# Row maxima of a local attention taken from fp32 scores in 64x96 tiles, in place of bf16 scores in 128x160 tiles

## The reference

```
WINDOW, HEADS, DIM_HEAD, QK_SCALE = 32, 16, 64, 8.0
...
mask = (it < jb) | (it > jb + w) | (jb == -1)
sim = einsum('bhwie,bhwje->bhwij', bq, bk2) * QK_SCALE
sim = where(mask, -finfo.max, sim)
attn = softmax(sim, -1)
out = einsum('bhwij,bhwje->bhwie', attn, bv2)
```

## Time and profile before

| what | value |
|---|---|
| median of 3 runs | 3442.39 us (3433.99 to 3449.18) |
| profiled execution, its own time | 3430.56 us |
| its span | 3428.4 us |
| mean granted TensorE clock | 0.939 |
| PE busy | 3294.6 us, 96% |
| DVE busy | 2253.3 us, 66% |
| ACT busy | 2308.7 us, 67% |
| POOL busy | 1170.0 us, 34% |

### The profile page before, as it was taken

How to read it: one execution, slowest core, us unless ns; L and a number is a source line. 1 busy time by engine, 2 the same in 40 slices (tenths; PEclk the granted TensorE clock), 3 DMA queues, 4 the chain that set the end, 5 groups by cost and what they waited for, 6 DMA issues and landing times.

```text
span 3428.4 us, 55664 instructions
## 1 busy us (share of the span) xinstructions
PE 3294.6 (96%) x17648; PEld 2094.4 (61%) x17648; DVE 2253.3 (66%) x3692; ACT 2308.7 (67%) x3969; POOL 1170.0 (34%) x1073
## 2 busy tenths in 40 slices
PE   5999899999999999999999999999999999999997
PEld 2444466666666666666666666666666666666664
DVE  5654476676666667667667667666766766766763
ACT  2543487777767767767767767777766777766773
POOL 2000143335433336333336333245332344333330
PEclk9965799999999999999999999999999999999997
DMA  2000010011100001100011100011100011100010
GB/s 74 1 1 1 13 44 35 34 41 42 46 36 33 34 35 50 47 30 37 34 37 51 44 33 37 31 43 47 43 33 31 37 47 43 45 31 31 37 36 20
DMA packets 101641, 121.85 MB, mean 36 GB/s; under 512 B 21972, under 2 KB 50770, under 8 KB 101458
## 3 DMA queue, kind: packets, MB, share of 16 engines
q1 hardware_dynamic: 101586, 121.15, 10.1%
HBM read 19.38 MB, written 1.05 MB: 6 GB/s over the span
## 4 chain that ended last, share of the span: by engine, by line
PE 86%; ACT 6%; DVE 5%; issue 3%; DMA 0%; SPq 0%; POOL 0%; DVEq 0%; ACTq 0%; POOLq 0%
PE ring L790 14%; PE ring L812 12%; PE ring L768 5%; PE bank L829 5%; PE ring L788 5%; PE ring L766 4%; PE ring L798 4%; PE ring L778 3%; PE bank L565 3%; PE ring L565 3%; PE bank L736 2%; PE ring L736 2%; PE ring L566 2%; PE ring L567 2%; PE bank L567 2%
## 5 line engine op out<-in xcount | busy, mean ns | idle before, releaser
L506 POOL TENSOR_TENSOR sq_lo<-sq_q,sq_hi 128x512 fp32r<-128x512 f32 x192 | 244.5, 1273 | 1500.0 <-ACT sq_hi L1009 1500.0
L790 PE MATMUL ring<-fin 64*128 64x160 f32 (+1 forms) x3072 | 608.0, 318 | 0.0
L1318 DVE TENSOR_REDUCE neg_max<-ring 128x2 bf16<-128x320 f32 x768 | 357.4, 489 | 265.7 <-PE ring L768 261.7
L812 PEld LDWEIGHTS ring<-probs_t,v_sb 128*128 128x128 f32 x3072 | 468.9, 199 | 72.9 <-issue 33.1
L790 PEld LDWEIGHTS ring<-fin 64*128 64x128 f32 x3072 | 440.5, 188 | 109.6 <-issue 4.8
L812 PE MATMUL ring<-probs_t,v_sb 128*128 128x160 f32 (+1 forms) x3072 | 506.1, 310 | 0.7 <-ACT probs_t L1033 0.7
L1024 ACT ACTIVATE neg_row<-ring 1x512 bf16<-1x512 f32 x384 | 225.1, 586 | 276.5 <-PE ring L778 271.8
L1033 ACT ACTIVATE probs_t<-ring 128x320 f32<-128x320 f32 (+1 forms) x768 | 284.1, 422 | 184.3 <-PE ring L798 184.3
L515 POOL TENSOR_TENSOR rot_k<-tc_k,ts_k 128x512 f32<-128x512 f32 x192 | 259.1, 1350 | 374.4 <-issue 374.4
L1328 DVE TENSOR_TENSOR o_feat<-ring,inv_sums 64x512 f32<-64x512 f32 x384 | 263.7, 687 | 168.4 <-ACT inv_sums L1045 165.5
L515 POOL TENSOR_TENSOR rot_q<-tc_q,ts_q 128x512 f32<-128x512 f32 x192 | 245.2, 1277 | 279.6 <-DMA ts_q<-sr_q 257.6
(11 more groups left out here) (185 smaller groups left out, 6050.3 us busy)
## 6 DMA issues: line engine op xcount, KB each, us to landing
ts_q<-sr_q SPq DMA_DIRECT2D x384, 128.0 KB, 2.0
ts_k<-sr_k SPq DMA_DIRECT2D x384, 128.0 KB, 2.0
w_raw<-in_L_ffn_Wqkv SPq DMA_DIRECT2D x48, 192.0 KB, 2.7
wo_sb<-in_L_ffn_Wo SPq DMA_DIRECT2D x6, 512.0 KB, 3.8
w_raw<-in_L_ffn_W SPq DMA_DIRECT2D x6, 341.0 KB, 3.0
rot_sb<-in_rotary SPq DMA_DIRECT2D x1, 1024.0 KB
out<-x_tok SPq DMA_DIRECT2D x16, 64.0 KB, 1.6
w_sb<-in_L_ffn_W SPq DMA_DIRECT2D x6, 128.0 KB
```

Of the source, the lines that this page charges most:

```text
L506: pool.tensor_tensor(sq_lo[:, i, :], sq[i][:], sq_hi[:, i, :].bitcast(F32), ALU.subtract).then_inc(s_sql[i], 1)
L790: pe.matmul(dst[:, at:at + q], k_fin[rows, p % 2, c * P:(c + 1) * P], q_fin[rows, p % 2, c * P:c * P + q], start=False, stop=False)
L812: mm = pe.matmul(dst[:, c * P:c * P + q], v_sb[:, c, p, h * DIM_HEAD:h * DIM_HEAD + P], probs_t[:, h, c * KEYS:c * KEYS + q], start=(c == ...
L1318: dve.tensor_reduce(neg_max[:, h, 2 * b:2 * b + 2], bank[2 + 2 * h + b][:, 0:2 * KEYS].rearrange("p (c k) -> p c k", c=2), AX_X, ALU.max, ...
```

## The change

The scores for the maxima are made from the fp32 q and k. The two casts and the bf16 copies go, with the semaphore pair `s_16`; `max_scores` waits for `s_fin`. The scores of a head lie in one bank of 384 columns in place of two of 320: each chunk of 128 queries is split into two blocks of 64, the first to output rows 0 to 63, the second to rows 64 to 127, and each block meets only the 96 keys it can see. The mask tensor is rebuilt for that shape, VectorE reduces once per head in place of twice, and `fin` gets 32 zero columns ahead of each k (a memset ahead of the layers).

```diff
@@ shape_constants
-    local = np.stack([np.where(seen & (j >= 0), 0.0, MASKED), np.where(seen, 0.0, MASKED),
-                      np.where(seen, 0.0, MASKED)], 1)
+    local = np.concatenate([np.where(seen & (j >= WINDOW - HALF_P * (i // HALF_P + 2 * c)), 0.0, MASKED)
+                            for c in range(CHUNKS)], 1)
...
@@ buffers (HALF_P = 64, REACH = 96, NEAR = 4 * REACH)
-        fin = sb("fin", [P, 4, TOK])
-        q_fin, k_fin = fin[:, 0:2, :], fin[:, 2:4, :]
-        q16 = sb("q16", [P, 2, TOK], BF16)
-        k16 = sb("k16", [P, 2, WINDOW + TOK], BF16)
+        fin = sb("fin", [P, 4 * TOK + 2 * WINDOW])
+        q_fin = fin[:, 0:2 * TOK].rearrange("p (i t) -> p i t", i=2)
+        k_fin = fin[:, 2 * TOK:].rearrange("p (i t) -> p i t", i=2)
...
@@ max_scores
-                    pe.wait_ge(s_16[0], n + 1)
-                    pe.wait_ge(s_16[1], n + 1)
+                    pe.wait_ge(s_fin[0], n + 1)
+                    pe.wait_ge(s_fin[1], n + 1)
...
-                for b in range(2):
-                    dst = bank[2 + 2 * h + b]
-                    pe.matmul(dst[:, 0:2 * KEYS], eye16, local_mask[:, b * KEYS:(b + 2) * KEYS], start=True, stop=False)
-                    for c in range(2 * b, 2 * b + 2):
-                        mm = pe.matmul(dst[:, (c % 2) * KEYS:(c % 2 + 1) * KEYS], q16[rows, p % 2, c * P:(c + 1) * P],
-                                       k16[rows, p % 2, c * P:c * P + KEYS], start=False, stop=(c % 2 == 1))
-                    mm.then_inc(s_s, 1)
+                pe.matmul(bank[2 + 2 * h][:, 0:NEAR], eye16, local_mask, start=True, stop=False)
+                for c in range(CHUNKS):
+                    for e in range(2):
+                        at = HALF_P * (2 * c + e)
+                        mm = pe.matmul(bank[2 + 2 * h][HALF_P * e:HALF_P * (e + 1), c * REACH:(c + 1) * REACH],
+                                       q_fin[rows, p % 2, at:at + HALF_P], k_fin[rows, p % 2, at:at + REACH],
+                                       start=False, stop=(c == CHUNKS - 1))
+                mm.then_inc(s_s, 1)
@@ turn_max
-                pe.wait_ge(s_mx, 4 * n + 2 * h + 2)
+                pe.wait_ge(s_mx, 2 * n + h + 1)
@@ turned_scores
-                        pe.matmul(dst[:, at:at + q], k_fin[rows, p % 2, c * P:(c + 1) * P],
+                        pe.matmul(dst[:, at:at + q], k_fin[rows, p % 2, WINDOW + c * P:WINDOW + (c + 1) * P],
...
@@ vector engine, ahead of the layers
-            dve.memset(k16[:, :, 0:WINDOW], 0.0).then_inc(v0, 1)
...
+            dve.memset(k_fin[:, :, 0:WINDOW], 0.0).then_inc(v0, 1)
@@ final
-                dst = (q_fin, k_fin)[i][:, p % 2, :]
+                dst = (q_fin[:, p % 2, :], k_fin[:, p % 2, WINDOW:])[i]
...
-                dve.wait_ge(s_fin[i], n + 1)
-                dve.tensor_copy(q16[:, p % 2, :] if i == 0 else k16[:, p % 2, WINDOW:], dst).then_inc(s_16[i], 1)
@@ maxima
-                for b in range(2):
-                    dve.wait_ge(s_s, 4 * n + 2 * h + b + 1)
-                    if b == 0 and not (isinstance(n, int) and n == 0):
-
-                        dve.wait_ge(s_tm, 2 * n - 1 + h)
-                    dve.tensor_reduce(neg_max[:, h, 2 * b:2 * b + 2],
-                                      bank[2 + 2 * h + b][:, 0:2 * KEYS].rearrange("p (c k) -> p c k", c=2),
-                                      AX_X, ALU.max, negate=True).then_inc(s_mx, 1)
+                dve.wait_ge(s_s, 2 * n + h + 1)
+                if not (isinstance(n, int) and n == 0):
+                    dve.wait_ge(s_tm, 2 * n - 1 + h)
+                dve.tensor_reduce(neg_max[:, h, :],
+                                  bank[2 + 2 * h][:, 0:NEAR].rearrange("p (c k) -> p c k", c=CHUNKS),
+                                  AX_X, ALU.max, negate=True).then_inc(s_mx, 1)
```

More of the change, by code:

```diff
@@ L34 @@
 KEYS = WINDOW + P
+HALF_P = P // 2
+REACH = HALF_P + WINDOW
+NEAR = CHUNKS * REACH
 FFN = int(D * 4 * 2 / 3)
@@ L72, in shape_constants @@
     i = np.arange(P)[:, None]
-    j = np.arange(KEYS)[None, :] - WINDOW
-    seen = (j <= i) & (j >= i - WINDOW)
-    local = np.stack([np.where(seen & (j >= 0), 0.0, MASKED), np.where(seen, 0.0, MASKED),
-                      np.where(seen, 0.0, MASKED)], 1)
+    near = (np.arange(P) % HALF_P)[:, None]
+    j = np.arange(REACH)[None, :]
+    seen = (j >= near) & (j <= near + WINDOW)
+    local = np.concatenate([np.where(seen & (j >= WINDOW - HALF_P * (i // HALF_P + 2 * c)), 0.0, MASKED)
+                            for c in range(CHUNKS)], 1)
     key, query = np.arange(P)[:, None], np.arange(KEYS)[None, :]
@@ L79, in shape_constants @@
     causal = np.where(np.arange(P)[None, :] <= i, 0.0, MASKED)
-    masks = np.concatenate([local.reshape(P, -1), turned, turned, causal, np.eye(P), causal.T], 1).astype(np.float32)
+    masks = np.concatenate([local, turned, turned, causal, np.eye(P), causal.T], 1).astype(np.float32)
     eye = np.eye(P, dtype=np.float32)
@@ L118, in build_program @@
         bank += [ctx.enter_context(nc.psum_tensor(f"bank{i}", [P, 512], F32))[:, :] for i in (6, 7)]
[L121 to L126, removed]
+        mask_sb = sb("mask_sb", [P, NEAR + 2 * KEYS + 3 * P], BF16)
+        local_mask = mask_sb[:, 0:NEAR]
+        local_mask_t = mask_sb[:, NEAR:NEAR + 2 * KEYS]
+        causal_mask = mask_sb[:, NEAR + 2 * KEYS:NEAR + 2 * KEYS + P]
+        eye16 = mask_sb[:, NEAR + 2 * KEYS + P:NEAR + 2 * KEYS + 2 * P]
+        causal_turned = mask_sb[:, NEAR + 2 * KEYS + 2 * P:NEAR + 2 * KEYS + 3 * P]
         ones16 = sb("ones16", [1, P], BF16)
@@ L191, in build_program @@
         values = sb("values", [P, NF, TOK])
-        mask_raw = gates[:].rearrange("p a t -> p (a t)")[:, 0:5 * KEYS + 3 * P]
+        mask_raw = gates[:].rearrange("p a t -> p (a t)")[:, 0:NEAR + 2 * KEYS + 3 * P]
         wkqv_sb = values[:, 0, 0:3 * P]
@@ L200, in build_program @@
         add_q = o_feat[:, 2:2 + GROUP, :]
-        add_k = fin
+        add_k = fin[:, 0:4 * TOK].rearrange("p (i t) -> p i t", i=4)
         qa = parts_sb
@@ L280, in build_program @@
         s_ve = [sem("v_even_out"), sem("v_odd_out")]
-        s_16 = [sem("q_rounded"), sem("k_rounded")]
         s_s = sem("rounded_scores")
@@ L1120, in _ @@
             dve.memset(wk_pad[:], 0.0).then_inc(v0, 1)
-            dve.memset(k16[:, :, 0:WINDOW], 0.0).then_inc(v0, 1)
             dve.memset(ones16[:], 1.0).then_inc(v0, 1)
             dve.wait_ge(s_const, 16 * CONST_LOADS)
-            dve.wait_ge(v0, 4)
+            dve.wait_ge(v0, 3)
             dve.tensor_copy(mask_sb[:], mask_raw).then_inc(v0, 1)
@@ L1134, in _ @@
             dve.tensor_copy(m_round[:], m_col[:]).then_inc(v0, 1)
+            dve.wait_ge(v0, 11)
+            dve.tensor_tensor(m_lo, m_col[:], m_round[:].bitcast(F32), ALU.subtract).then_inc(v0, 1)
             dve.wait_ge(v0, 12)
-            dve.tensor_tensor(m_lo, m_col[:], m_round[:].bitcast(F32), ALU.subtract).then_inc(v0, 1)
-            dve.wait_ge(v0, 13)
             for slots in v_slots[0] + v_slots[1]:
@@ L1141, in _ @@
             dve.memset(row_max[:], 0.0).then_inc(v0, 1)
-            dve.wait_ge(v0, 14)
+            dve.wait_ge(v0, 13)
             for slots in v_slots[0] + v_slots[1]:
                 dve.memset(slots.rearrange("p (h r) -> p h r", r=SLOT)[:, :, GLOBAL_DIM:GLOBAL_DIM + 1], 1.0)
-            k = 14
+            k = 13
             for i, (hi_row, lo_row) in enumerate(((M_HI_Q, M_LO_Q), (M_HI_K, M_LO_K))):
```

## The result

The changed kernel takes 3673.89 us, the median of 4 runs (3663.28 to 3685.86); the kernel before took 3445.78 in its 4. The ratio is 1.066, 95% interval 1.060 to 1.072. I had forecast 3456 us and a range up to 3512, so the time lies far outside. The side was right, the size was not. Each ratio in this text is taken of the executions without the slow ones on either side, so it is not the exact quotient of the medians beside it.

What follows compares the result with a forecast made beforehand. TensorE, busy 491 of 500 us, was taken as the bound. Terms of +42 (new block), +6 (half clock), -11 and -20 (`o_feat` waits, clock falls) and -3 (`neg_row`) gave +14 on 3442: 3456 us, range 3418 to 3512.

Steps and rivals of the forecast that it cites:

- The side: The whole kernel was forecast to get slower, 3456 us against 3442; slower by over 0.5% was given chance 0.53.
- At nothing: Items priced at zero: the wait for `s_fin`, the memset, the smaller mask, the first pair's casts, unchanged DMAs.
- the price of the forecast: TensorE's clock: a fall to half clock lasting 10.24 us was priced at 4.1 us.
- The new block: `max_scores` on TensorE: mask 0.27 plus products 0.81 us against 0.96 before, +0.11 us a head, +42 us over 384 heads.
- C: New products on TensorE: the two output halves take turns, 8 more places, +253 us, 3709 us; chance 0.08.
- D: New products on TensorE: weight loads are not hidden, 7 places longer by 0.053 us, +142 us, 3598 us; chance 0.05.
- VectorE's reduce: VectorE's reduce of 384 columns was to take 489 to 590 ns and stay hidden behind TensorE's work.
- The wait for `o_feat`: TensorE's 14 waits at L766 for the normed head were all to go without the casts, -11 us.
- The falls behind the weight split: Half clock behind the `o_feat` wait in five layers was to go, 5 x 4.1 = -20 us.
- The wait for `neg_row`: TensorE's 23 waits, ended by a ScalarE chain, were each to shrink by 0.11 us, -3 us; its clock fall stays.
- Rival E: Clock falls behind the `neg_row` waits go too, about -48 us, giving 3408 us; chance 0.10.
- Rival B: Clock falls behind the split stay (+20 us) or product pairs run one place late (+32); 3476 to 3508 us; chance 0.22.

Runs made afterwards that it cites:

- after_align: Changed kernel, TensorE's loop kept but its first instruction placed at the start of a block of 256 instructions; 3462.39 us, ratio 1.012 to the kernel before.
- after_slot64: Changed kernel with the first instruction of TensorE's loop placed 64 instructions behind the start of a block of 256; 3593.19 us, ratio 1.046.
- experiments 1 to 3: Changed kernel, loop straight: 3465.05 us; kernel before, 384 or 192 waits added: 3617.82, 3441.77; changed kernel, loop head at block start or 64 instructions on: 3462.39, 3593.19.
- before_pad384: Kernel before with 384 waits on a long-set semaphore spread over TensorE's loop body, no work added; 3617.82 us, ratio 1.046.
- Experiment 6: The change's halves apart: new tiles with bf16 copies kept, 3318.95 us; kernel before with fp32 operands in the old shape, 3757.11 us.
- fp32_wide: Kernel before without casts and bf16 copies, maxima scores from fp32 q and k in the old shape; 3757.11 us, ratio 1.081.
- after_hint: Changed kernel, TensorE's loop kept, with a prefetch hint for its backward branch; 3458.23 us, ratio 0.997.
- after_unroll: Changed kernel with TensorE's loop over the 22 middle bodies written out as straight code; 3465.05 us, ratio 1.012.
- bf16_tiles: Changed kernel with the bf16 copies, casts and semaphores put back, so bf16 products in the new tiles; 3318.95 us, ratio 0.957.

## Why the prediction was wrong

**The step that failed** is the one headed "At nothing". I listed waits, a memset and DMAs, and left out that 22 more matmuls and 22 more weight loads a pair stand in a loop body. This was a term of nothing in the sum, and it measured 212 us of the 225. I never looked at the loop as something that has a size. The page's row of queue 8 (30 packets for 22 turns) shows that the old loop stayed on the engine, so the row to ask from was there.

What it cost: `after_align` has every instruction of the changed kernel and its loop, and its layers took 2977.1 us, against 3189.1. The difference is 212 us. 73.5 us of it are the 41 waits for issue, mostly 2.2 to 2.5 us at the branch and 0.9 to 2.1 behind the first three products. The rest, 138 us, goes with the clock: over the layers the mean clock was 0.92 and not 0.97. In the trace's clock records that is 495 us at half clock and not 151, and 344 us at the price of the forecast (4.1 us for 10.24) are 138 us. The same two terms give 48 + 76 = 124 us for `after_slot64`, whose layers are 126.5 us longer than those of `after_align`.

**What is shown and what is inferred of the mechanism.** Shown: a cost of this kind comes with the address and the length of the loop, with the new tiles or without them, and is absent with all of them in another place or in straight code (experiments 1 to 3). In the costly cases 223 or 224 packets are fetched in place of 35, 189 more in 21 taken branches, 9 a turn. A packet is 16 KB (3.65 MB / 223). It holds some 256 instructions: straight code has 21 more turns than the loop, each of some 1710 instructions (70 fewer than in the loop: 62640 - 61099 over 22 turns), and it fetches 174 - 35 = 139 packets more, which makes 258 for each. The Trainium skill, "Advanced Engine Details and Errata", section "ISA Cache", gives TensorE 128 KB in lines of 16 KB, 256 instructions each. That makes 8 lines. The section adds "Only 2 cache lines!", which fits the 32 KB that it gives the other engines and not TensorE, where 7 or 8 stay in these runs. The runs agree as to the size of the lines. By 8 lines the loop of 1780 would seem to fit wherever it lies; without a hint 7 blocks stayed and 8 did not, with a hint 8 did (counted from where `head_slot` put the head; where the heads of the changed kernel and of `before_pad384` lie is not on record). The likeliest reading is that at the end of the loop the block behind it is fetched ahead, as a ninth, and pushes out the first, upon which each block of the turn is missing when it is wanted; 9 packets a turn fit that. The fetch ahead itself is not in any row, so this is inferred, and what the hint changes in it is open.

**The other steps, by the layers of `after_align` against before: +12.7 us, forecast +14.**

- *The new block.* Forecast 0.27 + 0.81. The straight code shows it at full clock:

```profile
1515.46 0.34 PE L766 MATMUL ring<-mask_sb 128*128 128x384 bf16 x1
1515.72 0.88 PE L770 MATMUL ring<-fin 64*64 64x96 f32 x16
1516.53 1.30 PE L815 MATMUL ring<-probs_t,v_sb 128*128 128x160 f32 x8
```

  1515.46 to 1516.53 is 1.07 us. The two halves run at once, 8 places for 16 matmuls, and the loads are hidden: rivals C and D are out. D came from a rule of the Trainium skill ("TensorE: Matmul & The Clock Gate", section "Part 3: Packing small matmuls — row/col tiling"), that a load overlaps a matmul only in another row group; these rows contradict it, as all 16 matmuls have the same rows. The same section also names a second way, a load into "the background weight buffer", which they don't contradict. At half clock the block is 1.95 us, from 2165.20 to 2167.15, as forecast. Experiment 6 found the same arithmetic right for two more shapes.
- *VectorE's reduce* took 558 ns, within the 489 to 590 given, and stayed hidden:

```profile
L1317 DVE TENSOR_REDUCE neg_max<-ring 128x4 bf16<-128x384 f32 x384 | 214.1, 558 | 679.4 <-PE ring L770 677.8
```

- *The wait for `o_feat`*, 10.9 us in 14 times, became 1.0 us in 2 in the changed kernel.
- *The falls behind the weight split* are gone. The kernel before has 23 stretches of half clock around its 23 waits for `neg_row` (133 us) and five of 10.2 us behind the wait for `o_feat`. `after_align` has none of those five; it has 21 around its 23 waits for `neg_row` (136 us).
- *The wait for `neg_row`*, 37.1 us, became 34.4: -2.7, forecast -3.
- *Rival E*, that a slightly shorter wait would spare falls, did not come: at 1.5 us 2 of 23 were spared, and the other 21 were longer on average, so nothing was won. `fp32_wide`, whose waits are 0.6 us, still has 15 behind them.
- *Rival B* is out in both parts: no place was late, and the falls at the split went.

That the side came out right was luck. The terms that I had leave the kernel near where it was, at ratios of 0.997 to 1.012, as `after_hint`, `after_align` and `after_unroll` show; what made it slower by 6.6% was the term that I did not have. The chances were also added up wrongly: by my own parts slower has 0.55 and within 0.5% has 0.33, in place of 0.53 and 0.35.

## What to carry to other kernels

Count the instructions between the branches of each engine's loop before and after an edit, fp32 matmuls as four records each, and look at the packets of the instruction queue. If a loop body nears eight blocks of 256, align its head (as long as it then fits 7 blocks) or give its branch a hint: here either line is worth some 6% and removes the waits at the branch. Bodies of more than 8 blocks were not run.

A change made of two parts should be priced in two parts. Here the tiles are worth 4% of the kernel, the fp32 operands take all of that and more, and the casts that they save lay beside other work. The version to keep is `bf16_tiles`, which beats both kernels.

## What the runs showed of the hardware that I had not expected

Moving a loop by 64 instructions changed the kernel by 3.8% (3462 to 3593 us) with not one instruction different. A missed fetch cost more through the clock than through the wait: 73.5 us of waits stood against 138 us of slower matmuls around them. And a branch hint did more than shorten the branch: it brought the packets of instructions from 223 down to 35, so that nothing was fetched in the turns at all.
